# The order of the first steps of a fused attention and expert kernel on VectorE, ScalarE and TensorE

## What is computed

```python
xn = _layernorm(x, axis=-1)
x = x + _L0_attn_ref(xn, W_qkv, W_out) + _L0_ffn_ref(xn, Wq, bq, ..., We, bexp)

# attention
q, k = rotary_embedding(q), rotary_embedding(k)
scores = jnp.where(tril, einsum('bqhd,bkhd->bhqk', q, k) * scale, -1e9)
out = softmax(scores) @ v @ W_out
# the small block ("ffn")
attn_out = softmax(einsum('bqhd,bkhd->bhqk', q, k) / sqrt(8)) @ v @ Wo + bo
x = x + layernorm(attn_out, g1, be1)
top_vals, top_idx = top_k(softmax(x @ Wg + bg), 2)
return x + layernorm(sum(top_vals * (x @ We + bexp)[top_idx]), g2, be2)
```

## Time and profile before

| | us |
|---|---|
| median of 3 runs | 1275.77 |
| lowest, highest | 1274.55, 1276.5 |
| the profiled execution's own time | 1276.25 |
| its span | 1274.5 |
| TensorE busy in the span | 1156.8 (91%) |
| VectorE, ScalarE, GpSimd busy | 926.7, 891.6, 817.6 |

### The profile page before, as it was taken

One profiled execution on the slowest core, in us unless ns is written; L12 is line 12 of the kernel. 1 busy time (PEld: TensorE's weight loads), 2 busy tenths in 40 slices (PEclk: granted clock), 3 DMA queues, 4 the chain that ended last, 5 costly groups with the idle time before them and its releaser, 6 DMA issues.

```text
span 1274.5 us, 25320 instructions
## 1 busy us (share of the span) xinstructions
PE 1156.8 (91%) x9387; PEld 737.4 (58%) x9387; DVE 926.7 (73%) x2329; ACT 891.6 (70%) x1841; POOL 817.6 (64%) x734
## 2 busy tenths in 40 slices
PE   3779999999999999999999999999999999899985
PEld 2354566656565565756656556655657566475553
DVE  8666487875878768795778758787677956778455
ACT  3577777587766867588775877668685786748750
POOL 3664774577755867468856768568675578636751
PEclk8799999999999999999999999999999999999988
DMA  5000100010000110001100110001100011000000
GB/s 143 34 34 18 42 34 18 25 50 35 26 25 18 51 42 26 21 30 51 43 9 34 38 39 34 18 26 51 43 26 18 26 51 43 10 32 20 34 18 8
DMA packets 34094, 42.87 MB, mean 34 GB/s; under 512 B 5678, under 2 KB 17200, under 8 KB 33972
## 3 DMA queue, kind: packets, MB, share of 16 engines
q1 hardware_dynamic: 30500, 38.31, 8.3%
q10 hardware_dynamic: 3472, 2.95, 0.8%
HBM read 5.60 MB, written 2.10 MB: 6 GB/s over the span
## 4 chain that ended last, share of the span: by engine, by line
PE 56%; DVE 15%; ACT 14%; POOL 6%; issue 6%; DMA 2%; SPq 0%; POOLq 0%; ACTq 0%; DVEq 0%
PE work L1271 7%; PE work L1185 7%; PE work L1286 6%; PE work L1298 5%; PE work L1187 5%; PE work L1186 5%; PE work L1348 5%; ACT fpt L856 5%; DVE fnmax L1043 4%; PE work L1314 4%; ACT pn L898 4%; DVE work L1145 3%; PE work L1323 3%; PE work L1338 3%; ACT pt L910 2%
## 5 line engine op out<-in xcount | busy, mean ns | idle before, releaser
L898 ACT ACTIVATE pn<-work,nmax 128x512 f32<-128x512 f32 (+3 forms) x512 | 265.3, 534 | 123.2 <-DVE nmax L1145 123.0
L757 POOL TENSOR_TENSOR raw<-raw,cos_t 128x512 f32<-128x512 f32 x128 | 164.1, 1282 | 289.4 <-DMA swapped<-raw 261.5
L1043 DVE TENSOR_REDUCE fnmax<-work 128x2 f32<-128x1024 f32 x256 | 301.9, 1218 | 47.0 <-PE work L1323 45.8
L1145 DVE CUSTOM_DVE_ANT_0 work<-work,causal 128x512 f32<-128x512 f32 (+3 forms) x512 | 236.0, 519 | 95.5 <-PE work L1271 94.6
L856 ACT ACTIVATE fpt<-work 128x1024 f32<-128x1024 f32 x256 | 252.4, 1029 | 52.7 <-PE work L1338 51.3
L1286 PE MATMUL work<-consts,pn 128*128 128x128 f32 x1280 | 173.0, 277 | 6.2 <-DVE fnmax L1043 4.0
L761 POOL TENSOR_TENSOR raw<-raw,swapped 128x512 f32<-128x512 f32 x128 | 163.9, 1280 | 10.0
L772 POOL TENSOR_TENSOR qk_l<-raw,qk_h 128x512 fp32r<-128x512 f32 x128 | 163.6, 1285 | 2.8
L1286 PEld LDWEIGHTS work<-consts,pn 128*128 128x128 f32 x1280 | 141.2, 141 | 41.7 <-DVE fnmax L1043 13.1
L758 POOL TENSOR_TENSOR swapped<-swapped,sin_t 128x512 f32<-128x512 f32 x128 | 164.2, 1283 | 0.0
L910 ACT COPY pt<-work 128x1024 f32<-128x1024 f32 x128 | 130.2, 1019 | 32.6 <-PE work L1286 32.1
(11 more groups left out here) (157 smaller groups left out, 2132.9 us busy)
## 6 DMA issues: line engine op xcount, KB each, us to landing
swapped<-raw SPq DMA_DIRECT2D x256, 128.0 KB, 2.0
x_in<-in_L_attn_x_dram SPq DMA_DIRECT2D x8, 256.0 KB, 3.6
out_dram<-x_in SPq DMA_DIRECT2D x8, 256.0 KB, 2.2
fpt<-in_L_attn_W_qkv_dram ACTq DMA_DIRECT2D x3, 512.0 KB, 5.9
pt<-in_L_ffn_We_dram ACTq DMA_DIRECT2D x1, 512.0 KB, 7.1
wout<-in_L_attn_W_out_dram ACTq DMA_DIRECT2D x1, 512.0 KB, 8.4
pt<-in_rope_dram ACTq DMA_DIRECT2D x1, 192.0 KB, 6.5
affine<-in_L_ffn_g_dram SPq DMA_DIRECT2D x2, 64.0 KB, 3.9
```

The costliest lines, as they stand in the source:

```text
L757: nc.gpsimd.tensor_tensor(raw[:, n % 3], raw[:, n % 3], cos_t[:], ALU.mult)
L898: ins = nc.scalar.activation(pn[:, h, PN_AT[j]:PN_AT[j] + n], bank_of(("sc", b, c, unit), h)[:, at:at + n], ACT.Exp, scale=-1.0, bias=nmax ...
L1043: nc.vector.tensor_reduce(fnmax[:, j, 2 * r:2 * r + 2, 0:1], bank_of(("fsm", b, g, j), 2 * r, 2).rearrange("p (f n) -> p f n", f=2), AX.X, ...
L1145: ins = nc.vector.tensor_tensor_reduce(out=scores, in0=scores, in1=causal[:, S - n:S], scale=-1.0 / math.sqrt(DH), scalar=3.0e38, op0=ALU.add,
```

## The change

Only numbers in `START`, `SHIFT` and `FIRST` change (the rest of the diff breaks long rows of the tables elsewhere). No step is added or taken away and none goes to another engine. GpSimd's and SP's lists stay as they are, and so do the transfers at the head of ScalarE's. A line of each table:

```diff
 START = {
-    "tb": [-347.661251],
+    "tb": [-573.664928],
 SHIFT = {
-    "ln": {1: -149.534351, 6: 14.649982},
+    "ln": {1: -14.661483, 6: 14.649982},
 FIRST = {
-    "xn": [-246.954742],
+    "xn": [-262.810963],
```

More of the change, by code:

```diff
@@ L58 @@
 START = {
[L59 to L63, removed]
-    "tb": [-347.661251],
[L65 to L72, removed]
+    "turn": [-394.037724],
+    "tt": [-484.125762],
+    "tab": [-163.729939],
+    "str": [-464.237636],
+    "strl": [-450.197654],
+    "tb": [-573.664928],
+    "qkb": [-408.077707],
+    "wh": [-324.997799, -284.680834, -244.363869],
+    "wl": [-422.117689, -337.877795, -239.597919],
+    "smh": [-264.522352],
+    "sml": [-295.757848],
+    "bia": [-281.717866],
+    "weh": [-183.888421],
+    "wel": [-155.358024],
     "ln": [-342.271788],
@@ L93 @@
         -144.817713, -127.497996, -123.99992, -117.808546, -117.135814, -112.502454, -109.587484, -99.434705],
[L94 to L97, removed]
+    "fexp": [-63.653581, -63.000896, -59.153534, -58.678651, -55.817139, -55.783707, -54.023713, -53.992146, -40.549729,
+        -32.140862, -15.961229, -15.238063, -11.376562, -5.442263, 17.13317, 17.734774, 19.366751, 19.805132, 23.753618,
+        25.175129, 30.526451, 30.877776, 42.501521, 42.775661, 46.620761, 46.978374, 54.263413, 56.998669, 68.262321,
+        68.73145, 73.854582, 73.883308],
     "fpv": [-210.629104, -209.890563, -209.395493, -206.093957, -147.740861, -147.573192, -144.756542, -131.5754,
@@ L157 @@
     "tq": [-203.516198, -148.934604, -126.83861, -117.798366, -109.456387, -93.573783, -82.94, -74.364791],
-    "tpe": [-39.309081, -29.149792, -0.647223, 1.317237, 22.287919, 30.131276, 39.579323, 42.0214, 69.422546,
-        72.697422, 78.316275, 80.6584, 88.083511, 91.586633, 99.409889, 101.707729],
+    "tpe": [-39.309081, -29.149792, -0.647223, 1.317237, 22.287919, 30.131276, 39.579323, 42.0214, 69.422546, 72.697422,
+        78.316275, 80.6584, 88.083511, 91.586633, 99.409889, 101.707729],
     "tqe": [-82.092567, -57.592391, -42.295327, -26.30228, -8.001158, 13.726925, 28.393263, 59.175223],
@@ L259 @@
     "rs0": [-1.401444],
-    "xn": [-246.954742],
+    "xn": [-262.810963],
     "xT": [-317.612733],
[L262 to L269, removed]
+    "xh": [-172.681497],
+    "xl": [-234.889533],
+    "fv": [-116.856626],
+    "fvc": [-72.023836],
+    "fqk": [-266.858401, -24.7422, -14.442461, -3.744268],
+    "fqkh": [-110.307559, -24.024679, -5.941804, -0.584486],
+    "fqkl": [-196.735275, -41.769451, -9.28883, -1.263711],
+    "fsm": [-197.817169, -173.818368, -146.693127, -60.166267, -3.447643, -8.741592, -16.861987, -13.00091, -7.482207,
         0.36522, -4.664974, -11.535928, -16.768964, -15.424425, -15.702452, -9.443807],
-    "fmax": [-170.387807, -169.719313, -164.096355, -138.381352, -65.74636, -66.316849, -62.547707, -49.103638,
+    "fmax": [-215.008566, -205.084438, -180.381921, -167.144126, -126.078, -114.061041, -94.311354, -81.209734,
         -37.703411, -36.488734, -31.878698, -31.374176, -29.978774, -25.985068, -28.958745, -24.246808, -11.329354,
@@ L275 @@
     "fmT": [-0.884423, -3.082854, -12.23953, 0],
-    "fsub": [-55.143385, -6.193732, 1.941914, 2.535849],
+    "fsub": [-64.183787, -6.193732, 1.941914, 2.535849],
     "fst": [-6.08239, -13.581924, -26.877253, -24.370466, -12.756922, -4.217907, -6.233826, -4.652733, -5.208069,
         -18.416785, -14.973197, -4.110382, -0.273899, -4.610461, -1.048526, -5.159652],
[L279 to L282, removed]
+    "fexp": [-17.084616, -15.720949, -15.424421, -14.956239, -16.344108, -12.790753, -12.848208, -10.748681, -0.624113,
+        -8.460598, -2.845827, -0.752992, -0.892369, -4.467677, -2.255918, -0.510762, 0.493029, 0.526811, -0.56167,
+        -0.592362, -2.581631, -1.853045, 0.105947, 0.707587, -2.111178, -1.074274, -7.224157, -6.473256, -8.3074, -7.988375,
+        -1.765784, -0.604923],
     "fpv": [-28.747596, -29.28431, -3.986806, -5.9038, -4.282424, -4.12889, -5.265203, -16.448562, -10.848831,
@@ L310 @@
     "store": [-20.832021],
-    "proj": [-292.062732, -10.870984, 0.468632, -2.001313, -20.456277, -7.818018, 0, 0.103058, -5.564903, -16.079855,
+    "proj": [-260.203948, -86.589858, 0.468632, -2.001313, -20.456277, -7.818018, 0, 0.103058, -5.564903, -16.079855,
         -15.167499, -4.678059, 0.003981, -2.080292, -0.823034, -12.011642],
-    "raw": [-42.676351, -17.393796, -9.795251, -12.64905, -7.667494, 3.721634, -10.867326, 2.136104, -0.954049,
+    "raw": [-123.909711, -45.609975, -9.795251, -12.64905, -7.667494, 3.721634, -10.867326, 2.136104, -0.954049,
         -0.021905, -0.851768, 1.150397, 1.665846, -9.907534, -7.160971, -7.095138],
```

6 lines of the change are left out of this document (3 added, 3 removed), and 36 rows, old and new, of tables (FIRST, START).

## The result

The changed kernel took 1280.15 us in the median of 17 runs (1276.71 to 1283.98), the kernel before 1276.2 us in 17 runs beside them on the same chip. The ratio is 1.0027, 95% interval 1.0017 to 1.0038: slower by 0.27%, or 3.4 us (2.2 to 4.8). The two medians are 3.95 us apart, which lies inside that interval. The profiled execution took 1279.38 us with a span of 1277.6 us; the one before had 1276.25 and 1274.5. TensorE's mean granted clock was 0.975, before 0.977.

The account below looks back on a forecast made before the run. It took a tight TensorE chain to bound the long run and VectorE to decide the head. Gains and losses, summed at `fst` 0.0.2, made 3.7 us on the 1275.77 us median: 1279.5 us, range 1275.4 to 1283.0.

Parts of the forecast that it names:

- To the first maxima: Head: earlier `xn` meets the `value_bias` wait at `tb`; first maxima at 21.4 in place of 23.88, 2.5 us ahead.
- The first contention: Between maxima 0.0.0 and 0.0.1: `wl` 1 waits 0.75 us on VectorE for GpSimd's second operation.
- The second contention: Behind maxima 0.0.1: `sml` falls into GpSimd's `lo` and waits about 1.0 us; `bia` done at 30.5.
- `fv` to the maxima 0.0.3: TensorE: `fv` from 30.5 takes 2.8 us at the slow pace; maxima 0.0.3 at 35.3, 1.2 us behind.
- The statistics: VectorE, behind maxima 0.0.3: batch 1's statistics add 2.15 us ahead of `fqkl` 0.1.
- Behind it: After the statistics: `fqkl` 0.1 to 41.2, `wel` 1.2 us, group 1's maxima at 43.1, `fst` 0.0.2 at 47.85, 3.7 us behind.
- The shift reaches the end: Behind `fst` 0.0.2 engines follow each other, so its 3.7 us delay should reach the end whole.
- no contention: Rival: VectorE operations in the head never wait for GpSimd; 1.8 us less, +1.9, 1277.7 us; chance 0.18.
- The load comes sooner: Rival: `tb` doesn't wait for `value_bias`, `fqk` 0.0 starts at 12.4; +1.3, 1277.1 us; chance 0.03.
- The clock gives it back: Rival: full clock at `fv` and `proj` 0.0.1 and in the 50.8 to 56.0 stretch; -0.2, 1275.6 us; chance 0.13.
- Faster: Rival: VectorE never waits for GpSimd and both dense TensorE stretches get full clock; -2.0, 1273.8 us; chance 0.08.
- more: Rival: one more dense TensorE stretch further on at 1.2 GHz, up to 2.6 us; 1282.1 us; chance 0.10.

Follow-up runs that it names:

- c_two_moves: The changed kernel with `sml` and `bia` moved ahead of the first maxima and `wel` into the pause ahead of maxima 0.0.3; ratio to the kernel before 0.9994.
- a_ln1_ahead: The changed kernel with batch 1's statistics moved back ahead of the first maxima; ratio to the kernel before 1.0041.
- b_head_delay: The kernel before with three useless reductions of 1024 columns on VectorE ahead of batch 0's `xn`; ratio to the kernel before 1.0040.
- b_ln1_late: The kernel before with only batch 1's statistics moved, behind the maxima 0.0.3 as in the change; ratio to the kernel before 0.9997.
- a_tb_behind_fqk: The changed kernel with `fqk` 0.0 ahead of `tb` on TensorE; ratio to the kernel before 1.0048.

## Why the prediction was right, step by step

The forecast was 1279.5 us (1275.4 to 1283.0), slower the likeliest; measured 1280.15. In the head it was 3.7 us, and 3.1 were measured there. Step by step:

- **To the first maxima: right, nearly to the digit.** `xn` at 8.30 (8.4), the load landed at 14.4 (14.3), `fqk` 0.0 from 14.88 to 17.83 (14.8 to 17.7, at the slow pace), `fqkh` 17.83, `fqkl` 19.31, maxima 21.42 (21.4). One wait was left out: `qkb` waits for `bg_rows` as well, and starts its work on the columns at 15.67 and not at 15.1. It lay under the wait for `fqkh` and cost nothing.
- **The first contention stood at the wrong place.** `wl` 1 was to wait 0.75 us for GpSimd. The first `rope` waited not for `tab` but for the exchange of `raw`'s halves by DMA, so it began at 22.58 and not at 22.0; `wl` 1 had VectorE and the memory at 23.69 and GpSimd's next operation was stretched instead, 2.26 us. The step "GpSimd starts when `tab` is done" was wrong. The 0.75 us were not paid on VectorE there; that the sum still came out is luck, since the contentions further on were larger than it had them.
- **The second contention: right in kind, larger in size.** 1.0 us was put on `sml`; it was 1.44 us, most of it on `biases` (1.63, by itself 0.75). A third one, at `wel` (1.81, in c_two_moves 1.22), wasn't in the sum: 0.6 us. Together 2.0 us where 1.8 stood.
- **`fv` to the maxima 0.0.3: right.** `fv` at 30.25 (30.5), twelve matmuls in 2.8 us as taken, maxima 0.0.3 at 35.21 (35.3).
- **The statistics: wrong, the term that failed.** 2.15 us were put on the path. They took 1.5, since the last of their rows is 0.27, where before it was 1.00 and ended with GpSimd's first operation, begun at 22.67. And of these 1.5 nothing counts, as a_ln1_ahead shows. What stands in their place is a step that the prediction left out: `fqk` 0.1, which was behind `proj` 0.0.1 and ahead of `fsm` 0.0.3 before and is now behind `fsm` 0.0.3, so that `fqkh` 0.1 starts 3.9 us later (37.47, before 33.60). From maxima 0.0.3 to `fqkl` 0.1 this makes 3.77 us, for which the sum had 4.5. No run puts `fqk` 0.1 back ahead of `fsm` 0.0.3, so its part is read from the traces and not tested.
- **Behind it.** `fqkl` 0.1 at 38.98 (39.8), maxima 0.1.0 at 42.63 (43.1), `fst` 0.0.2 at 47.29 (47.85): +3.1 in place of +3.7. The 0.7 too much between maxima 0.0.3 and `fqkl` and the 0.5 too little at `wel` partly cancel, so the sum is better than its steps. One row was misread: the chain doesn't go on from `fst` 0.0.2 without VectorE, since the maxima at 48.41 are on it. They moved by the same 3.1 us, so it cost nothing.
- **The shift reaches the end: right as far as 308 us, and with luck behind it.** To 308 us the change and b_head_delay carry it whole: the drops of their granted clock lie where the kernel before has them, only later by the shift. That needn't be so. In b_ln1_late the shift is 0.2 at `fst` 0.0.2, 1.8 at 102 us and -1.0 at 240 us. Behind 308 us single steps of 1.5 us go both ways in the change as well, and that they come to zero in the profiled execution (3.1 at the end) is chance.

Of the rivals: *no contention* falls (1.44 us measured). *The load comes sooner* falls, since it landed after 6.3 us. The Trainium skill, DMA: Bandwidth & Descriptors, section "Anatomy of one DMA", fits its 2.0 us to transfers that GpSimd issues, and this one is SP's. What a sooner landing would have given wasn't run: a_tb_behind_fqk lets `fqk` 0.0 start without waiting (first maxima 0.3 us behind, not 2.4 ahead), but it also puts `tb` later, and `qkb` would have waited for `bg_rows` until 15.67 in any case. *The clock gives it back* falls: the twelve matmuls of `fv` ran at the slow pace, and so did those behind 53.7 us. *Faster* and *more* fall too: neither all the gains nor a net loss to the clock came.

The Trainium skill, SBUF — State Buffer, section "SBUF: two separate sides", agrees with the runs in kind: both engines are held up, and the pair 1.63 and 0.75 appears and vanishes with GpSimd's work. Its rule names VectorE operations with two SBUF inputs and those in a 2-port perf mode. The cast has one input and was 0.83 with GpSimd at work and 0.42 without; that it runs in such a mode, no view here shows.

## What to carry to other kernels

Look for the light work of the engine that decides, and place it where that engine waits in any case: two such moves, read off one timeline's pauses, took back 3.7 of the 4.2 us lost at the maxima 0.1.0 and 2.8 of the 3.1 at `fst` 0.0.2, while the early `xn` alone only brought a new wait. Ahead of costing a moved step at its own length, ask what its follower waits for next: the statistics were worth nothing, because ScalarE's `fqkh` was ready just when they ended. And compare variants where their lists become the same, not tens of microseconds further on, where a drop of the clock can hide half of a gain. Where two engines' lists meet at the memory, the sum of the contention can be bounded, its place hardly.
